# A graph network on one core: shorter edge records, runs of 136 words, and two norm blocks cut into seven pieces

## What is computed

```
L0, three times:  m = ffn(concat(h[dst], h[src], e16), w1);  m = ffn(m, w2)
                  h = h + ffn(concat(h, segment_sum(m, dst)), wu)      ffn(x, w) = relu(ln(x @ w + b))
L1:               z = concat(h[src], h[dst], e32)
                  g = segment_sum(sigmoid(z @ Wf + bf) * softplus(z @ Ws + bs), src)
                  h + (g - mean(g)) * rsqrt(var(g) + eps) * gamma + beta   (statistics over the nodes)
L2:               segment_sum(h[src], dst)
L3:               concat(h, segment_sum(concat(h[src], e32) @ W1 + b1, dst)) @ W2 + b2
```

## Time and profile before

| | |
|---|---|
| median of 3 runs | 10311.94 us (10299.15 to 10319.37) |
| the profiled execution | 10303.77 us |
| its span in the trace | 10302.0 us |
| busy: TensorE, VectorE, ScalarE, GpSimd | 75%, 65%, 60%, 68% |
| TensorE weight loads | 64% |
| DMA | 2335.5 MB, mean 227 GB/s |

### The profile page before, as it was taken

One profiled execution on the slowest core, in us unless ns is written; L12 is line 12 of the kernel. 1 busy time (PEld: TensorE's weight loads), 2 busy tenths in 40 slices (PEclk: granted clock), 3 DMA queues, 4 the chain that ended last, 5 costly groups with the idle time before them and its releaser, 6 DMA issues. The chain is left out here.

```text
span 10302.0 us, 371177 instructions
## 1 busy us (share of the span) xinstructions
PE 7708.6 (75%) x123397; PEld 6597.2 (64%) x123398; DVE 6703.4 (65%) x15839; ACT 6194.6 (60%) x16024; POOL 7045.8 (68%) x9555
## 2 busy tenths in 40 slices
PE   7666666646578999889998899977777756455666
PEld 5444444434467888788887888866666646445666
DVE  7444444456635999737886378863499993664697
ACT  2555555546636999728996289962388852442343
POOL 2777777777746888657885478850188855774676
PEclk9999999985589999899998999989999989657887
DMA  6222222249999888597775977769988859667987
GB/s 250 67 67 68 70 66 66 67 150 327 326 274 312 273 278 274 171 363 253 240 239 143 372 245 239 239 109 384 369 264 257 255 158 360 208 206 237 317 288 218
DMA packets 1408418, 2335.54 MB, mean 227 GB/s; under 512 B 311979, under 2 KB 826300, under 8 KB 1381310
## 3 DMA queue, kind: packets, MB, share of 16 engines
q1 hardware_dynamic: 1078046, 1293.68, 40.3%
q0 software_dynamic: 217824, 515.78, 17.0%
q10 hardware_dynamic: 112320, 523.03, 12.7%
HBM read 1381.15 MB, written 905.59 MB: 222 GB/s over the span
## 5 line engine op out<-in xcount | busy, mean ns | idle before, releaser
L639 POOL DMA_INDIRECT by_src<-sort_rec,slots x1560 | 1543.9, 990 | 650.8 <-issue 650.8
L1328 POOL DMA_INDIRECT NEAR<-spread_f,gather_ids_l x1368 | 1375.9, 1006 | 252.2 <-issue 180.2
L1453 ACT ACTIVATE z_l<-z_l,sizes_l 128x64 f32<-128x64 f32 x5472 | 1376.9, 342 | 0.1
L773 PE MATMUL bank<-hots_t 104*128 104x512 bf16 (+3 forms) x1568 | 614.4, 467 | 720.4 <-ACT junk L598 720.2
L773 PEld LDWEIGHTS bank<-hots_t 104*128 104x128 bf16 x1568 | 218.3, 139 | 1020.0 <-ACT junk L598 832.5
L1536 PE MATMUL bank<-wm_diag,zr_t_l 128*128 128x128 f32 x5472 | 795.6, 288 | 2.6 <-issue 2.6
L1536 PEld LDWEIGHTS bank<-wm_diag,zr_t_l 128*128 128x128 f32 x5472 | 664.8, 192 | 158.7 <-issue 158.7
L1490 PE MATMUL bank<-m_l,hot_wide_l 128*128 128x64 f32 x5472 | 740.7, 278 | 0.0
L1183 POOL COPY unit_near_a<-NEARB 128x192 bf16 x1368 | 417.4, 349 | 424.9 <-PE bank_bf L1168 209.9
L1515 PE MATMUL bank<-NEARB,hot_t_l 128*128 x16416 | 644.5, 194 | 46.3 <-DMA hot_t_l<-dst_hots_t 15.6
L1490 PEld LDWEIGHTS bank<-m_l,hot_wide_l 128*128 128x128 f32 x5472 | 664.3, 192 | 0.0
(11 more groups left out here) (392 smaller groups left out, 27495.3 us busy)
## 6 DMA issues: line engine op xcount, KB each, us to landing
spread_f<-unit_rows_a ACTq DMA_DIRECT2D x342, 512.0 KB, 5.9
hot_t_l<-dst_hots_t SPq DMA_DIRECT2D x456, 256.0 KB
hot_wide_l<-dst_wide SPq DMA_DIRECT2D x456, 256.0 KB
unit_hot_a<-src_hots_t SPq DMA_DIRECT2D x342, 256.0 KB, 4.0
dst_hots<-NEAR SPq DMA_DIRECT2D x228, 256.0 KB
dst_hots_t<-hot_t_l SPq DMA_DIRECT2D x228, 256.0 KB
dst_wide<-hot_wide_l SPq DMA_DIRECT2D x228, 256.0 KB
NEAR<-dst_hots SPq DMA_DIRECT2D x456, 128.0 KB
```

The costliest lines, as they stand in the source:

```text
L639: pool.indirect_dma_start(out=by_src, out_offset=bass.IndirectOffsetOnAxis(ap=slots[h][:, j:j + 1], axis=0), in_=rec[h][:, j, :], in_offse ...
L773: pe.matmul(to, lhsT=cols[:, t * P:width], rhs=cols[:, 0:width], start=True, stop=False, skip_group_check=True)
L1328: pool.indirect_dma_start(out=far_in[h % WA][:, g * GT:(g + 1) * GT, :].rearrange("p j f -> p (j f)"), out_offset=None, in_=spread_f, in_o ...
L1453: last = act.activation(z[h % WA][:, t, :], z[h % WA][:, t, :], ACT.Relu, scale=sizes[h % WA][:, 2, 0, t:t + 1])
```

## The change

**Records.** A record of an edge has 51 words: source, target, the place of its run, 16 and 32 features. The integer copies of source and target, the words for a constant one and zero, and the word for the run's own place go; with them ScalarE's copy L623, which is one of four per step of the sort, and the 12 copies that set the constants ahead of its loop.

**Runs.** A row of `by_dst` has 136 words: 4 x 32 edge columns, 4 targets, the own place, 3 unused. It is put together in a buffer `run` of its own (a ring of 4), and the scatter takes it from there. ScalarE's copy of the 32 columns, which went to a buffer for TensorE, goes into `run`, and TensorE turns it from there. VectorE writes the own place and the four targets (one more small copy). SyncE's load of the records waits for the readers of the record buffer four steps back, no longer for the scatter; ScalarE and VectorE wait for that scatter ahead of their first write into `run`. The table is filled with such rows.

**Readers.** The first message pass and the last sum pass load rows of 136 words. In the last sum pass the column of ones stands in the bf16 tile of the third part, and the products with the first and third part change places.

**Norm blocks.** A function `settle(name, batch)` makes both. After the sum over the nodes it works on seven pieces of 7 windows (448 columns), with VectorE, ScalarE (squares, roots, two of the three bf16 parts) and GpSimd (the addition of H and beta, zeroing) in a pipe of three ticks. Scale and mean are read from PSUM. Each block becomes a stage with semaphores of its own.

The records and runs, and the copy that goes from the sort's step:

```diff
-RW = 56
-SRC_F, DST_F, SRC_I, DST_I, HERE, THERE = range(6)
-A16, A32 = 6, 6 + E16
-ONE, NIL = A32 + E32, A32 + E32 + 1
+SRC_F, DST_F, HERE = range(3)
+A16, A32 = 3, 3 + E16
+RW = A32 + E32
+RUN_DST, RUN_THERE = GT * E32, GT * E32 + GT
+RUN_W = 136
...
-        by_dst = dram("by_dst", [2 * NS, RW])
+        by_dst = dram("by_dst", [2 * NRUN, RUN_W])
...
-                            act.activation(rec[h][:, :, SRC_I:DST_I + 1].bitcast(I32), both_i[:, cols, :],
-                                           ACT.Copy).then_inc(copied[h], 1)
```

In `move_runs`, the lists of SyncE, ScalarE, GpSimd and VectorE in this order:

```diff
-                            at_least(sp, moved[h], 16 * MG * (nth - 1))
+                            at_least(sp, s["past"], n - W)
+                            at_least(sp, s["here"], n - W)
+                            at_least(sp, s["targets"], n - W)
+                            at_least(sp, s["key"], n - W)
+                            at_least(sp, s["e16"], n - W)
+                            at_least(sp, s["e32"], n - W)
                             sp.dma_start(rec[h][:], runs_in[:, bass.ds(MG * st, MG), :]).then_inc(rec_in[h], 16)
...
-                            at_least(act, s["e32_turned"], n - 2)
-                            act.activation(e32_flat[h % 2][:].rearrange("p g (j f) -> p (g j) f", f=E32),
-                                           words[:, :, A32:A32 + E32], ACT.Copy).then_inc(s["e32"], 1)
+                            at_least(act, s["e32_turned"], n - W)
+                            at_least(act, moved[h], 16 * MG * (nth - 1))
+                            act.activation(run[h][:, :, 0:GT * E32].rearrange("p g (j f) -> p g j f", f=E32),
+                                           rec[h][:].rearrange("p g (j f) -> p g j f", f=RW)[:, :, :, A32:A32 + E32],
+                                           ACT.Copy).then_inc(s["e32"], 1)
...
-                        pool.wait_ge(s["key"], n)
-                        pool.wait_ge(s["e16"], n)
+                        pool.wait_ge(s["targets"], n)
                         pool.wait_ge(s["e32"], n)
...
-                                in_=rec[h][:, g, :], in_offset=None).then_inc(moved[h], 16)
+                                in_=run[h][:, g, :], in_offset=None).then_inc(moved[h], 16)
...
-                            dve.tensor_copy(rec[h][:, :, THERE].bitcast(I32), own[k][:]).then_inc(s["noted"], 1)
+                            at_least(dve, moved[h], 16 * MG * (nth - 1))
+                            dve.tensor_copy(run[h][:, :, RUN_THERE].bitcast(I32), own[k][:]).then_inc(s["noted"], 1)
+                            dve.tensor_copy(run[h][:, :, RUN_DST:RUN_DST + GT],
+                                            rec[h][:].rearrange("p g (j f) -> p g j f", f=RW)[:, :, :, DST_F]).then_inc(s["targets"], 1)
```

The new `settle`: VectorE's part ahead of the scaling, its tick without most of its waits (part(k) is the piece of k ticks ago), and ScalarE's tick:

```diff
+                        dve.tensor_reduce(bn[:, 0, :], ACC[:].rearrange("p w f -> p f w"), AX, ALU.add).then_inc(s["node_sums"], 1)
...
+                        for i in range(NWC):
+                            dve.tensor_tensor(ACC[:, rows_of(i), :], ACC[:, rows_of(i), :], over(mean_ps),
+                                              ALU.subtract).then_inc(s["acc_centre"], 1)
...
+                        for i in range(NWC):
+                            dve.wait_ge(s["acc_square"], i + 1)
+                            dve.tensor_reduce(stage[:, i, 0:D], S[:, rows_of(i), :].rearrange("p w f -> p f w"), AX,
+                                              ALU.add).then_inc(s["part"], 1)
...
+                        if (i := part(1)) is not None:
+                            dve.wait_ge(s["square"], i + 1)
+                            dve.tensor_reduce(size[:, rows_of(i)], S[:, rows_of(i), :], AX, ALU.add).then_inc(s["size"], 1)
+                        if (i := part(0)) is not None:
+                            if batch:
+                                dve.tensor_tensor(ACC[:, rows_of(i), :], ACC[:, rows_of(i), :], over(scale_ps),
+                                                  ALU.mult).then_inc(s["scaled"], 1)
...
+                            dve.tensor_tensor(X[:, rows_of(i), :], X[:, rows_of(i), :], ACC[:, rows_of(i), :],
+                                              ALU.add).then_inc(s["x_next"], 1)
+                        if (i := part(1)) is not None:
...
+                            dve.reciprocal(size[:, rows_of(i)], size[:, rows_of(i)]).then_inc(s["rec"], 1)
...
+                            dve.scalar_tensor_tensor(out=H[:, rows_of(i), :], in0=H[:, rows_of(i), :], scalar=0.0,
+                                                     in1=by_window(size[:, rows_of(i)]), op0=ALU.max,
+                                                     op1=ALU.mult).then_inc(s["h"], 1)
+                        if (i := part(0)) is not None:
...
+                            dve.tensor_reduce(mean[:, rows_of(i)], X[:, rows_of(i), :], AX, ALU.add).then_inc(s["x_sum"], 1)
...
+                        if (i := part(2)) is not None:
...
+                            dve.tensor_tensor(NEARB[:, rows_of(i), 2, 0:D], S[:, rows_of(i), :], NEARB[:, rows_of(i), 1, 0:D],
+                                              ALU.subtract).then_inc(s["last"], 1)
...
+                            dve.tensor_tensor(S[:, rows_of(i), :], H[:, rows_of(i), :], NEARB[:, rows_of(i), 0, 0:D],
+                                              ALU.subtract).then_inc(s["rest"], 1)
...
+                        if (i := part(1)) is not None:
+                            act.wait_ge(s["size"], i + 1)
+                            act.activation(size[:, rows_of(i)], size[:, rows_of(i)], ACT.Sqrt, bias=eps[:],
+                                           scale=1.0 / D).then_inc(s["root"], 1)
+                        if (i := part(2)) is not None:
+                            act.wait_ge(s["rest"], i + 1)
+                            act.activation(NEARB[:, rows_of(i), 1, 0:D], S[:, rows_of(i), :], ACT.Copy).then_inc(s["middle"], 1)
+                        if (i := part(1)) is not None:
+                            act.wait_ge(s["h"], i + 1)
+                            act.activation(NEARB[:, rows_of(i), 0, 0:D], H[:, rows_of(i), :], ACT.Copy).then_inc(s["top"], 1)
+                        if (i := part(0)) is not None:
+                            act.wait_ge(s["centre"], i + 1)
...
+                            act.activation(S[:, rows_of(i), :], H[:, rows_of(i), :], ACT.Square).then_inc(s["square"], 1)
...
+        with new_stage():
+            settle("bn", True)
...
+        with new_stage():
+            settle("ln", False)
```

More of the change, by code:

```diff
@@ L604, in tick @@
                             h, st, n, nth = p
[L605 removed]
+                            if h == 0 and not (isinstance(nth, int) and not 2 <= nth <= NFILL + 1):
                                 fill_dst(nth - 2)
@@ L854, in move_runs @@
             e16_ps, e32_ps = banks[4:6], banks[2:4]
-            s = {n: sem(f"move_{n}") for n in ("ids", "past", "here", "noted", "aimed", "next", "own", "key", "hot",
-                                               "turned", "hot_t", "e16", "e32", "e16_turned", "e32_turned", "e16_side", "e32_side", "at")}
+            s = {n: sem(f"move_{n}") for n in ("ids", "past", "here", "noted", "targets", "aimed", "next", "own", "key",
+                                               "hot", "blank", "turned", "hot_t", "e16", "e32", "e16_turned", "e32_turned", "e16_side", "e32_side", "at")}
             written = [sem(f"move_written{k}") for k in range(W)]
@@ L950, in _ @@
                 def _(pool):
+                    for h in range(W):
+                        pool.memset(run[h][:, :, RUN_DST:], 0.0).then_inc(s["blank"], 1)
                     pool.iota(ids_i[:], pattern=[[P, MG]], base=NRUN, channel_multiplier=1).then_inc(s["ids"], 1)
@@ L2319, in sum_pass @@
             steps = NG // UG
-            s = {n: sem(f"{name}_{n}") for n in ("ids", "acc_ps", "whole", "rest", "second", "last", "rest_e", "last_e")}
+            s = {n: sem(f"{name}_{n}") for n in ("ids", "acc_ps", "whole", "rest", "second", "last", "ones_e", "rest_e", "last_e")}
             acc_added = [sem(f"{name}_acc_added{g}") for g in range(UG)]
@@ L2390, in _ @@
                 def _(dve):
+                    if with_edges:
+                        for k in range(2):
+                            dve.memset(last_e[k][:, :, E32:], 1.0).then_inc(s["ones_e"], 1)
+                        dve.wait_ge(s["ones_e"], 2)
                     def tick(part):
```

233 lines of the change are left out of this document (120 added, 113 removed).

## The result

| | before | after |
|---|---|---|
| median of 4 runs each, us | 10308.6 | 10205.7 |
| lowest to highest, us | 10299.2 to 10319.4 | 10201.6 to 10212.3 |
| ratio, 95% interval | | 0.9898 (0.9886 to 0.9910) |
| profiled execution's span, us | 10302.0 | 10201.8 |

What follows compares the result with a forecast made beforehand. GpSimd was taken to pace sort and move, ScalarE and TensorE the first message pass, VectorE the last sum pass and norms. Terms -10 - 1 - 3 - 2 - 1 - 1 - 27 = -45 from 10303.8, plus 8.1: 10267 us; range 10215 to 10305.

Steps and rivals of the forecast that it cites:

- passes otherwise as before: Sign of being right: apart from the stages with stated changes, passes keep their times; the gate pass had no term.
- Rival 1: Move: VectorE's comparisons, released by scatter landings, always fall into the same gap, so the lock goes; 10209 us, 12%.
- Rival 2: Move: every step has a scatter starting right behind a comparison, 1.1 us of lock for 0.53; slower, 10335 us, 8%.
- the move's forecast of -3: Move of the runs: random comparison offsets shorten the lock by 0.03 us in 114 steps; bounds -61 and +65 us.
- Rival 3: Move: it waits for bytes, so it shrinks with them by 77 us; 10193 us, 7%.
- Sort: Sort: one ScalarE copy fewer lets comparisons start sooner, -10 us; constants gone, -1; smaller rows 0; bounds -29 to +63.
- Norms: Both norm blocks: seven pipelined pieces, -16.9 us with batch statistics and -10.2 without, -27 together; bounds -32 and 0.
- GpSimd zeroes the sums beside it: Norm block without batch statistics: GpSimd's zeroing runs alongside, with no cost entered for it.
- Rival 4: Norm blocks: nine ticks with their waits eat the 27 us, so no change; 10294 us, 15%.
- Last pass: Last sum pass: same VectorE subtractions and products, 0; a smaller first load, -1 us.
- The first message pass: First message pass: 139 KB a step for 229, hidden behind ScalarE and TensorE; -1 us, bounds -10 and +10.

Runs made afterwards that it cites:

- before_apart: Kernel before, with GpSimd's half of the third bf16 piece in the gate pass waiting for VectorE's half: 10252.7 us, ratio 0.9941.
- data_only: Changed kernel with the norm blocks of before, so the new records and runs alone: 10229.1 us, ratio 0.9918.
- 2 or 14 memsets: Kernel before plus that many one-column VectorE memsets ahead of the gate pass's loop: 10252.7 and 10256.4 us; with 7, 10326.9 us.
- after_best: Changed kernel plus the gate pass's wait for VectorE's half, and the zeroing of the sums moved to the sum pass before: 10203.8 us.
- norms_only: Kernel before with the two norm blocks by seven pieces and nothing else: 10292.0 us, ratio 0.9977.

## Why the prediction was wrong

- **The step that failed** is one sentence: "passes otherwise as before". Code that the diff leaves alone was priced at nothing. The gate pass, 1005 us long, was not in the sum, not among the rivals and not in the range, and it gave 60.4 us. The runs put in its place a pass with two rhythms: the two halves' meeting is the price (56 us, 978.9 for 922.7 in before_apart), the records and runs bring the gain (data_only, 921.5), and a shift of VectorE's instructions by itself can do the same (2 or 14 memsets: 59 us off the pass; 7: 18 us on). The prediction had the row that could have warned it: the earlier trace rows shows GpSimd idle for 58.1 us before `gate_rest` in the kernel before. It was read for its 1044 ns only. After, that wait is 10.1 us.
- **Bounds.** Rival 1 (10209) names the right time for a wrong reason: the lock in the move did not let go. Its landing near the result is chance. Rival 2 needs 0.90 us of lock a step. The move has 504.6 - 456 x 0.967 = 63.7 us in 114 steps, 0.56, for 0.53 before. Both are refuted, and the move's forecast of -3 was measured as +0.8, the same within its scatter: kernels with the old move took 639.0 to 643.7, those with the new one 637.6 to 643.3.
- **Rival 3**, bytes. In the move 284 GB/s for 322, a DMA share of 0.92 where 0.84 was forecast, and not 1 us less: the move does not wait for bytes. The page of the Trainium skill named there (DMA: Bandwidth & Descriptors, section "How a descriptor splits into AXI transactions") stays unweighed, as a stage that does not wait for bytes can't show what a read at an odd start costs.
- **Sort**: -11 forecast, -11.6 measured, of which some 4 come with a scatter of 967 ns instead of 971, which kernels of before show as well (data_only, at 971, takes 2009.8 us for 2017.7). The mechanism (the copy, not the bytes) is shown; its size is 7 to 9, and that the sum came out at 11.6 is luck in part.
- **Norms**: block with statistics 58.6 us for a forecast 56.1, tick 5.02 for 5.0; scaling begins 19.7 us in, for 18.7. The other: tick 4.37 for 4.34, block 36.9 for 32.8. Most of the 4.1 are a lock that the forecast priced at nothing, "GpSimd zeroes the sums beside it": a multiplication of 7 columns waits 2.56 us for the memset's end (after_best). Rival 4 is refuted: norms_only is faster, 0.9977.
- **Last pass**: -1 forecast, -7.7 measured with spread and output. The three stages together take 905.2 to 908.1 us in the six kernels with small runs and 909.1 to 916.5 in the ten with large ones, so the gain comes with the runs, and its size lies anywhere from 1 to 11 us. The gathers take 602.2 us from first to last for 606.1 (small runs 601.3 to 603.8, large ones 602.7 to 608.2). Their DMA share is 0.84 for 0.89. That this is from fewer late transfers is argued, not shown; no run took it apart.
- **The first message pass** was forecast at -1 with bounds of 10. First to last gather of all message passes takes 3590 to 3610 us in the ten kernels with the old runs and 3588 to 3593 in the six with the new ones; the profiled before is the fastest of the old ones. So the change may be worth up to about 10 us here, which that one profile hides.

What stays open: why VectorE stops at the turn-over, what in its instructions' place sets the stop's length, and which difference of the changed kernel keeps its pass fast. Also why its half, started 0.53 to 0.6 us behind `gate_rest`, ends 0.25 us inside GpSimd's instead of before its start, as 0.42 us would have it. That the wait removes this is shown; the course of the meeting is not.

## What to carry to other kernels

A pass that two engines pace together can have a fast and a slow rhythm, and even two empty instructions ahead of its loop can switch them: compare such passes stage by stage before crediting an edit, and test with a handful of empty instructions ahead of the loop. Where one instruction shows two durations in its source line (418/786/939), look at what the other engine does beside it; one wait that keeps the two apart can be worth more than the edit under study. In a sum of terms, give untouched passes that show such a row a term of their own, with bounds on both sides.

## What the hardware showed that was not expected

- The Trainium skill (SBUF — State Buffer, section "SBUF: two separate sides") has VectorE and GpSimd shut each other out for a whole instruction when VectorE reads two inputs from SBUF beside a GpSimd operation that reads SBUF, or runs in a mode that takes both ports. For the memset the trace agrees: VectorE's multiplication beside it takes 2.73 us for 0.17 and ends with the memset (9263.77 and 9263.74); which mode it ran in no trace shows. In the gate pass, where both halves read SBUF, the measurement differs: both are stretched together, 0.42 to 0.8 and 0.62 to 0.72 us, and they overlap in the record.
- TensorE's granted clock was 1.00 (2.4 GHz) in the sort of the profile before and 0.50 (1.2 GHz) in that of after the earlier trace rows, with TensorE busy 1264 and 1259 us and the sort no slower: GpSimd, which paces it, waits for TensorE in neither, and VectorE's wait for its look-up is 320 and 318 us in all. Between executions of one kernel the mean clock was 0.81 or 0.91 (10203.5 and 10201.6 us of the changed kernel).
